# Fused cross attention and non-local block: the transposed probabilities kept in block order, their split in pieces of 1024 elements

## What is computed

```python
# layer 0: attention, softmax over the key positions m
q = einsum('bcn,dc->bnd', x, Wq) + bq            # 64 wide
k = einsum('bcn,dc->bdn', ctx, Wk) + bk
v = einsum('bcn,dc->bdn', ctx, Wv) + bv          # 512 wide
attn = softmax(einsum('bnd,bdm->bnm', q, k), axis=2)
x = einsum('bcm,bnm->bcn', v, attn) + x
# layer 1: products of 1x1 convolutions, no softmax
W = einsum('bnc,bcm->bnm', theta(x), phi(ctx)) / 1024
y = einsum('bnm,bmc->bnc', W, g(ctx))
out = batchnorm(w(y)) + x
```

## Time and profile before

| what | value |
|---|---|
| runs | 1123.3, 1126.97 and 1127.23 us; median 1126.97 us |
| profiled execution, first to last instruction | 1122.5 us (its own device time is not recorded; the lowest run is 0.8 us above this span) |
| granted TensorE clock, mean | 0.993 |
| TensorE matmuls busy | 1061.0 us, 95% of the span |
| VectorE, ScalarE, GpSimd busy | 708.3, 468.6, 298.7 us (63%, 42%, 27%) |
| the hardware DMA queue | 35.0% of 16 engines' span |

### The profile page before, as it was taken

How to read it: one execution, slowest core, us unless ns; L and a number is a source line. 1 busy time by engine, 2 the same in 40 slices (tenths; PEclk the granted TensorE clock), 3 DMA queues, 4 the chain that set the end, 5 groups by cost and what they waited for, 6 DMA issues and landing times.

```text
span 1122.5 us, 13860 instructions
## 1 busy us (share of the span) xinstructions
PE 1061.0 (95%) x5144; PEld 889.3 (79%) x5144; DVE 708.3 (63%) x905; ACT 468.6 (42%) x802; POOL 298.7 (27%) x198
## 2 busy tenths in 40 slices
PE   5999999999799998999989999899998999989998
PEld 4788878887688876888768887688876888768886
DVE  6884377735777357673577726777277663777635
ACT  7653444425334253343534335443354433544231
POOL 0311252123421234112351134401344013440130
PEclk9999999999999999999999999999999999999999
DMA  8335241351414514145142442324423244232412
GB/s 276 102 81 174 78 172 39 101 181 57 151 38 108 174 57 151 40 116 164 61 146 51 113 156 72 136 54 113 152 76 132 59 113 148 76 131 66 116 45 75
DMA packets 80626, 122.05 MB, mean 109 GB/s; under 512 B 13104, under 2 KB 46384, under 8 KB 80560
## 3 DMA queue, kind: packets, MB, share of 16 engines
q1 hardware_dynamic: 80560, 121.17, 35.0%
HBM read 70.79 MB, written 16.78 MB: 78 GB/s over the span
## 4 chain that ended last, share of the span: by engine, by line
PE 72%; DVE 11%; DMA 7%; issue 5%; ACT 3%; POOL 1%; SPq 0%; DVEq 0%; ACTq 0%
PE pG L545 31%; PE pG L464 11%; PE pG L455 10%; DMA out_dram<-xr 6%; PE pG L556 6%; DVE xr L857 4%; PE pG L484 4%; DVE xr L852 3%; PE pM L524 2%; PE pM L533 2%; PE pS L495 2%; DVE qs L756 1%; PE pT L497 1%; PE pT L495 1%; PE pS L497 1%
## 5 line engine op out<-in xcount | busy, mean ns | idle before, releaser
L545 PE MATMUL pG<-pt,vT 128*128 128x512 f32 x1536 | 352.6, 390 | 0.3 <-DVE pt L807 0.3
L545 PEld LDWEIGHTS pG<-pt,vT 128*128 128x128 f32 x1536 | 287.3, 188 | 59.4 <-issue 0.5
L886 POOL TENSOR_TENSOR xms<-xr,xms 128x512 fp32r<-128x512 f32 x64 | 94.2, 1487 | 338.0 <-ACT xms L693 338.0
L455 PE MATMUL pG<-wv,x2s 128*128 128x512 f32 x768 | 179.8, 391 | 0.7 <-DVE wv L715 0.7
L455 PEld LDWEIGHTS pG<-wv,x2s 128*128 128x128 f32 x768 | 143.0, 188 | 30.3 <-DVE wv L715 1.1
L836 DVE SCALAR_TENSOR_TENSOR xr<-pG,cl,xr 128x512 f32<-128x512 f32 x64 | 48.0, 750 | 164.2 <-PE pG L545 163.5
L464 PE MATMUL pG<-x2Ts 128*128 128x256 f32 (+2 forms) x768 | 129.8, 327 | 0.0
L464 PEld LDWEIGHTS pG<-x2Ts 128*128 128x128 f32 x768 | 119.2, 192 | 9.5
L878 POOL TENSOR_TENSOR x2Ts<-x2T_f,x2Ts 128x512 fp32r<-128x512 f32 x64 | 91.0, 1450 | 122.8 <-ACT x2Ts L640 122.8
L807 DVE TENSOR_TENSOR pt<-mv,pt 128x512 fp32r<-128x512 f32 x128 | 80.9, 688 | 47.2 <-ACT pt L670 47.2
L882 POOL TENSOR_TENSOR ys<-yf,ys 128x256 fp32r<-128x256 f32 x32 | 31.2, 975 | 285.0 <-ACT ys L661 285.0
(11 more groups left out here) (102 smaller groups left out, 1307.3 us busy)
## 6 DMA issues: line engine op xcount, KB each, us to landing
mv<-tp SPq DMA_DIRECT2D x512, 64.0 KB, 2.0
st<-in_ctx_dram SPq DMA_DIRECT2D x32, 512.0 KB, 6.2
st<-in_x_dram SPq DMA_DIRECT2D x32, 512.0 KB, 4.4
x2T_f<-in_ctx2T_dram SPq DMA_DIRECT2D x32, 512.0 KB, 5.8
xr<-in_x_dram SPq DMA_DIRECT2D x64, 256.0 KB, 3.5
out_dram<-xr SPq DMA_DIRECT2D x64, 256.0 KB, 2.5
wv_f<-in_wvT_dram SPq DMA_DIRECT2D x4, 256.0 KB, 7.7
wpg_f<-in_wpgT_dram SPq DMA_DIRECT2D x1, 1024.0 KB, 6.0
```

The costliest lines, as they stand in the source:

```text
L455: last = mm(bank, x2s[:, l, c, 128 * m:128 * m + 128], wv[:, r, c, :], start=(c == 0 and n == 0), stop=(c == 3 and n == 2))
L545: last = mm(bank, vT[:, l, m, 128 * c:128 * c + 128], pt(h)[:, r, m, :], start=(m == 0 and n == 0), stop=(m == 7 and n == 2))
L886: done(tt(xms(h)[:, c, LO, :], xr[c][:, :], xms(h)[:, c, HI, :].bitcast(F), ALU.subtract), "xlo")
```

## The change

`pt` gets the shape [128, 2 parts, 4 query tiles t, 4 blocks j, 8 key blocks u, 32 queries n], the order in which the moved blocks already lie. A step T covers 2 tiles t and 2 blocks j: for each t that is 512 elements in one run, on both the read and the write side. So one instruction of 1024 elements takes the place of two of 512, on ScalarE and on VectorE. The matmuls of PV now stream, for key block m, 16 runs (4 t by 4 j) of 32 elements; one run begins 256 elements behind the one before. The order of the columns is the same as before, and PSUM is written as before. The memory that each tile takes is unchanged, as are the tables of the order.

```diff
-        pt1 = at("pt1", [128, 2, 8, 512], R, rb)
+        pt1 = at("pt1", [128, 2, 4, 4, 8, 32], R, rb)
-        pt0 = at("pt0", [128, 2, 8, 512], R, rc)
+        pt0 = at("pt0", [128, 2, 4, 4, 8, 32], R, rc)
         def moved(i):
 
             j = i % 2 * 2
-            return [mv(i // 2)[:, t, j:j + 2, :].rearrange("p j (u n) -> p u j n", u=8) for t in range(2)]
+            return mv(i // 2)[:, :, j:j + 2, :].rearrange("p t j n -> p t (j n)")
 
         def pt_half(i, part):
-            n = 256 * (i // 2 % 2) + 64 * (i % 2)
-            return [pt(i // 4)[:, part, :, n + 128 * t:n + 128 * t + 64].rearrange("p u (j n) -> p u j n", j=2)
-                    for t in range(2)]
+            t, j = i // 2 % 2 * 2, i % 2 * 2
+            return pt(i // 4)[:, part, t:t + 2, j:j + 2, :, :].rearrange("p t j u n -> p t (j u n)")
...
-                        last = mm(bank, vT[:, l, m, 128 * c:128 * c + 128], pt(h)[:, r, m, :],
+                        last = mm(bank, vT[:, l, m, 128 * c:128 * c + 128],
+                                  pt(h)[:, r, :, :, m, :].rearrange("p t j n -> p (t j) n"),
                                   start=(m == 0 and n == 0), stop=(m == 7 and n == 2))
...
-                for k in range(2):
-                    last = act(pt_half(t, HI)[k], moved(t)[k], ACT.Copy)
-                done(last, "Thi")
+                done(act(pt_half(t, HI), moved(t), ACT.Copy), "Thi")
...
-                for k in range(2):
-                    last = tt(pt_half(t, LO)[k], moved(t)[k], pt_half(t, HI)[k].bitcast(F), ALU.subtract)
-                done(last, "Tlo")
+                done(tt(pt_half(t, LO), moved(t), pt_half(t, HI).bitcast(F), ALU.subtract), "Tlo")
```

## The result

The changed kernel takes 1139.97 us (median of 4 runs, 1135.91 to 1141.33) against 1127.1 us before (4 runs): a ratio of 1.0106, with a 95% interval of 1.0079 to 1.0133. The change makes the kernel about 1.1% slower, 12.9 us by the medians. I had forecast no change, and the time lies 3 us above the range. Measured again on another occasion it was 1.0125 (1.0100 to 1.0149).

The account below looks back on a forecast made before the run. TensorE's matmul stream was taken to bound the kernel. TensorE 0, T work -0.3 and rest 0 took the median of 1126.97 us to 1126.7, rounded to 1126.5, with a range of 1120 to 1137 us.

Parts of the forecast that it names:

- What bounds the kernel: Whole kernel: TensorE's matmuls, busy 95% of the span, set the time; its wait for `pt` is only 0.3 us.
- ScalarE and VectorE: T steps: 64 larger instructions replace 128, saving 12.2 us on ScalarE and 10.1 on VectorE, hidden behind TensorE.
- Rival D: T steps: larger pieces save nothing on ScalarE and VectorE, time unchanged at 1127 us; chance 0.08.
- the 0.3 us of batch 0: TensorE's one wait for `pt`, in batch 0: the only part of the T saving forecast to reach the end.
- TensorE: PV's 1536 matmuls: reading 16 runs of 32 elements costs 0, between bounds of 0 and 307 us.
- Rival A: Every PV matmul: each jump costs TensorE a cycle, 6.3 ns per matmul, 9.6 us in all, 1136.6 us; chance 0.13.
- the two-cycle price: PV matmuls: the first rival's variant with two cycles per jump instead of one, giving 1146 us.
- Rival B: PV matmuls: a moving operand with jumps streams at half rate, 307 us more, 1434 us; chance 0.02.
- Rival C: T steps: the saving on ScalarE or VectorE reaches TensorE, giving about 1115 to 1117 us; chance 0.11.
- The rule of the Trainium skill: SBUF reads of PV's operand: full speed if two accesses share a 16-byte line, so runs of 32 cost nothing.

Follow-up runs that it names:

- e13: The changed kernel itself, measured again on one chip beside e14: median 1141.07 us, ratio 1.0125 to the kernel before.
- e14: The changed kernel with each T step in two instructions of 512 elements again: median 1141.32 us, ratio 1.0123 to the kernel before.
- e4: The kernel before with PV's moving operand read in 128 runs of 4 elements instead of one of 512: 1172.93 us in one run.
- e12: The kernel before with each T step in four instructions of 256 elements instead of two of 512: median 1130.44 us, ratio 1.0032.
- e11: The kernel before, `pt` in its old shape, each T instruction taking one query tile and all four blocks j (1024 elements): 1176.88 us, ratio 1.0451.

## Why the prediction was wrong, point by point

- *What bounds the kernel.* Right: TensorE's stream sets the time, and what the PV matmuls gained in length, 14.9 us, came out nearly in full (12.9 us by the first medians, 13.8 by those of e13).
- *ScalarE and VectorE.* Right: 1053 and 1217 ns per instruction, against 1051 and 1218; VectorE's mean wasn't that of L730. Rival D fell. The saving was hidden but for the 0.3 us of batch 0, as I had put it (e13 against e14).
- *TensorE.* This is the step that failed: "I take 0, the end that the rows with real jumps lie at". The rows were of ScalarE and VectorE, and they say nothing of TensorE. (I also misread one of them: `khi` is written in one run, and it is its source `kf` that is read in runs of 32.) One difference was in hand and I did not weigh it: these engines took about 1 ns per element on those rows, while TensorE takes a column every 0.44 ns (226.7 / 512). An engine that asks for its next element more than twice as often might be held up by a pattern that the others don't notice; that this is the reason wasn't tested. The measured price is 10.0 ns per matmul in the long stretches and 14.9 us in sum, where the prediction had 0.
- *Rival A* had the place, the sign and the argument that there is no slack in PV; its size was off: 6.3 ns and 9.6 us where 10.0 ns and 14.9 us were measured. Its law is wrong too. It had one cycle for each jump, 0.417 ns; 7 jumps cost nothing, and 127 cost 29.1 ns and not 53. Its chance of 0.13 was too low, since no row bounded TensorE's price. The range reached only to its price at one cycle; the two-cycle price, 1146 us, stood in the text, and a range up to it would have held the time.
- *Rival B* fell: even runs of one line of 16 bytes (e4) stream at 255.8 ns and not at half rate.
- *Rival C* fell: e13 and e14 have the same time. Its argument that T stands in front of evacuations on VectorE is right, but it works only the other way: more T work (e12) makes TensorE wait for an evacuation of Y, and less T work finds no wait to shorten.
- *The rule of the Trainium skill*, "Advanced Engine Details and Errata", section "Memory Cachelines": SBUF accesses at full speed with two or more on the same 16-byte line. The trace disagrees for TensorE's moving operand of float32r: runs of 32 elements are eight whole lines and cost 10.0 ns, and runs of 4 are one whole line and cost 29.1 ns in each matmul. The measurement decides: two accesses on a line are not enough here. The rule on PSUM in the same section was not tried, since PSUM was written in one run in every kernel.

## What to carry to other kernels

Where TensorE sets the time, lay out the moving operand for it and let ScalarE or VectorE bear the rearranging, above all where their time is hidden: here 12 and 10 us saved on them bought nothing that could be measured, and 10 ns in each of 1536 matmuls cost 1.1 to 1.3%. With 512 float32r columns, up to 8 runs of 64 elements were free and 16 runs of 32 were not, so a layout that keeps 8 runs of 64 costs TensorE nothing; whether it would spare the other engines anything wasn't tried. Look also at which evacuations stand behind a piece of work in an engine's queue: in e11 TensorE waited for those and not for the tile, and in e12 for more of them than for the tile. Don't read the price of an access pattern on one engine off the rows of another; where no row shows it, bound it from the side of the engine whose time is the bound.

## What the runs showed of the hardware that was not expected

One 512-column matmul after another, in ns from start to start, by the number of runs of its moving operand: 1, 2 and 8 runs 226.7; 16 runs 236.7 at 256 and at 1024 bytes from run to run; 32 runs 240.0 at 128 bytes and 242.4 at 512; 128 runs 255.8. With 256 columns: 119.4 in one run, 121.1 in 8 and in 16 runs. The law behind it stays open.

The other thing is TensorE's clock after the wait for `qs`. A timeline of TensorE in e14 and in the kernel before shows that wait and the first matmul behind it, in batch 3; then come the same of the changed kernel in batches 6 and 7, and its clock just after the wait in batch 3 (from:to, length, busy times, clock, the DMAs):

```profile
455.15 0.77 PE L494 MATMUL pS<-khi,qs 128*128 128x512 f32 x1 [3.07 <-DVE qs L756]
```

```profile
448.11 0.47 PE L495 MATMUL pS<-khi,qs 128*128 128x512 f32 x1 [3.03 <-DVE qs L756]
```

```profile
871.89 0.77 PE L494 MATMUL pS<-khi,qs 128*128 128x512 f32 x1 [2.32 <-DVE qs L754]
...
1013.36 0.47 PE L494 MATMUL pS<-khi,qs 128*128 128x512 f32 x1 [3.08 <-DVE qs L754]
```

```profile
454.00:456.00 2.00, 2.00 (x11) 1.61 (x10) 1.97 (x3) 0.63 (x3) 2.00 (x3) 1.00 0.00 0
```

In batch 3 the changed kernel was granted 1.00, 2.4 GHz, where the kernel before had 0.50, 1.2 GHz, at the same place behind a wait of about the same length, 2.71 us against 3.03. There the kernel before still ran its first matmuls at the upper level. In e14, behind 3.07 us of idling, the first one already shows 0.77 us instead of 0.47. The length of the wait alone doesn't decide: the changed kernel has 0.77 us behind 2.32 us in batch 6, and 0.47 us behind 3.08 us in batch 7. Which it is differs from batch to batch and between executions, and with it the matmuls of S and G: the 192 wide ones of G average 393 ns in the changed kernel's first profile, 403 in its second (e13) and 419 in e14, for the same instructions. From e13's profile to e14's the span grows by 6.8 us; the wide matmuls of G are busy for 2.8 us more and those of S for 5.0. So runs of one kernel spread over some microseconds (1134.6 to 1147.92 us for e14).
